# Moving the gating sort, its search and two copies in a convolution, attention and gating kernel

## The reference, cut to what matters

```
x = x + conv(groupnorm(x), w)
t = tokens(x)
# attention: 5000 nodes, 80000 random edges, 8 heads of 8
score = exp(clip(sum(k[src] * q[dst]) / sqrt(8), -5, 5))
t = t + segsum(v[src] * score, dst) / (segsum(score, dst) + 1e-6)
# gating: 8192 tokens, 262144 random edges, 4 heads x 4 experts
h = x @ W_gat;  e = leaky_relu(a_src[src] + a_dst[dst]);  alpha = softmax of e over each dst
agg = segsum(h[src] * alpha, dst);  gate = softmax(top2(mean_heads(layernorm(agg))))
t = t + sum_e gate[e] * (gelu(t @ W1[e] + b1[e]) @ W2[e] + b2[e])
```

## Time and profile before

| | |
|---|---|
| median of 3 executions | 2664.83 us |
| profiled execution, its own time | 2667.64 us |
| profiled execution, span of its instructions | 2665.8 us |
| VectorE busy | 1932.1 us (72%) |
| GpSimd busy | 1769.0 us (66%), issuing DMAs |
| TensorE busy | 1203.0 us (45%) |
| ScalarE busy | 535.9 us (20%) |

### The profile page before, as it was taken

The page is one execution under the profiler, slowest core; times in us unless marked ns, Lnnn a source line. Parts: engine busy times, 40 slices in busy tenths (PEclk is TensorE's granted clock), DMA queues, the critical chain, the costliest instruction groups (busy, mean ns, idle before and its releaser), DMA issues.

```text
span 2665.8 us, 34021 instructions
## 1 busy us (share of the span) xinstructions
PE 1203.0 (45%) x12499; PEld 1007.2 (38%) x12499; DVE 1932.1 (72%) x3127; ACT 535.9 (20%) x640; POOL 1769.0 (66%) x1690
## 2 busy tenths in 40 slices
PE   3874000000001001010214399589889898898286
PEld 2532000000000000000113255379889898887266
DVE  7588596988687878787888501168888888888356
ACT  1010002222222223131201011222222222222121
POOL 0001877777777777774677677777777777777470
PEclk9976555555555555555555555579989899899658
DMA  9500213233333333231222706112121222221101
GB/s 299 193 1 23 72 38 106 86 118 101 98 105 93 107 94 115 86 116 50 70 75 51 97 6 186 23 25 25 24 40 25 39 25 25 40 25 24 30 9 33
DMA packets 145715, 186.75 MB, mean 70 GB/s; under 512 B 84845, under 2 KB 103983, under 8 KB 139167
## 3 DMA queue, kind: packets, MB, share of 16 engines
q1 hardware_dynamic: 91494, 121.12, 14.6%
q0 software_dynamic: 54080, 63.61, 13.9%
HBM read 97.32 MB, written 87.32 MB: 69 GB/s over the span
## 4 chain that ended last, share of the span: by engine, by line
POOL 60%; issue 20%; DVE 10%; PE 6%; DMA 1%; ACT 1%; SPq 1%; POOLq 0%; DVEq 0%
POOL arena L729 56%; DVE arena L1359 7%; PE psum L933 2%; POOL d_adseed L816 2%; POOL d_qseed L753 1%; PE psum L1095 1%; SPq L569 1%; DVE arena L1362 1%; PE psum L1126 1%; PE psum L1011 1%; DVE psum L1761 1%; PE psum L1023 1%; ACT arena L1201 0%; DVE arena L1782 0%; DVE arena L1764 0%
## 5 line engine op out<-in xcount | busy, mean ns | idle before, releaser
L1359 DVE TENSOR_TENSOR arena<-arena 128x512 f32<-128x512 f32 (+18 forms) x1347 | 802.8, 635 | 160.7 <-ACT arena L1165 53.1
L729 POOL DMA_INDIRECT arena<-d_h,arena x668 | 696.4, 1042 | 203.7 <-issue 203.4
L729 POOL DMA_INDIRECT arena<-in_kv,arena x640 | 648.1, 1013 | 199.0 <-issue 194.5
L1050 PE MATMUL psum<-arena 128*128 128x128 bf16 x10080 | 613.6, 224 | 92.6 <-DVEq L1969 90.6
L1050 PEld LDWEIGHTS psum<-arena 128*128 128x128 bf16 x10080 | 600.1, 100 | 97.2 <-DVE arena L1362 94.9
L849 PE MATMUL psum<-arena 128*128 128x128 f32 (+3 forms) x402 | 90.0, 391 | 1100.2 <-DVEq L1435 1004.1
L849 PEld LDWEIGHTS psum<-arena 128*128 128x128 f32 (+3 forms) x402 | 68.7, 202 | 1122.7 <-DVEq L1435 1019.3
L1362 DVE TENSOR_SCALAR arena<-arena 128x512 bf16<-128x512 f16 (+9 forms) x1067 | 339.6, 376 | 67.7 <-ACT arena L1265 24.6
L1359 DVE TENSOR_TENSOR arena<-psum,arena 128x512 f32<-128x512 f32 (+2 forms) x179 | 167.2, 942 | 207.8 <-PE psum L1011 202.6
L729 POOL DMA_INDIRECT arena<-d_adst,arena x40 | 54.4, 1360 | 257.5 <-DVEq L1606 245.6
L1761 DVE TENSOR_TENSOR_SCAN psum<-psum,arena 128x1024 f32<-128x1024 f32 x40 | 91.9, 2298 | 137.0 <-ACT arena L1188 136.0
(11 more groups left out here) (184 smaller groups left out, 1385.5 us busy)
## 6 DMA issues: line engine op xcount, KB each, us to landing
d_gs<-arena SPq DMA_DIRECT2D x32, 768.0 KB
d_as<-arena SPq DMA_DIRECT2D x20, 1152.0 KB, 4.5
d_qseed<-arena SPq DMA_DIRECT2D x5, 4096.0 KB, 29.8
arena<-d_qseed SPq DMA_DIRECT2D x20, 1024.0 KB, 6.0
arena<-d_h,arena POOLq DMA_INDIRECT x668
arena<-in_kv,arena POOLq DMA_INDIRECT x640
d_adseed<-arena SPq DMA_DIRECT2D x1, 4096.0 KB, 29.4
arena<-d_adseed SPq DMA_DIRECT2D x17, 128.0 KB
```

The lines of the kernel that those rows point to most:

```text
L729: return pool.indirect_dma_start(out, None, table, bass.IndirectOffsetOnAxis(index[:, t:t + 1], 0))
L1050: last = nc.tensor.matmul(ps[2 + turn_of(b, m)][:, k * PICK_W:(k + 1) * PICK_W], pick_hot[turn_of(b, m)][:, t, k * P:(k + 1) * P], h_split ...
L1359: return V.tensor_tensor(o, a_, b_, op)
```

## The change

1. `SORT_EACH` goes from 14.5 to 22.0 and `LAY_TAKES` from 4.5 to 9.0, so that the sort ends before `lay` of chunk 18; the step `sorted` (unpack the list, histogram, running counts) stands there now, on VectorE and TensorE.
2. SyncE stores the gating list right after its loop, ahead of the last two chunks' rows; inside the loop it loads the next indices after `a_used` alone, and waits for `a_rows_set` and stores rows after that.
3. GpSimd does groups 0 and 1 of the search (32 of 64 gathers) ahead of its wait for the last attention rows.
4. In the attention loop ScalarE copies k into `a_prod` and v into `a_msg` feature-major; VectorE's products read these, and `a_used` is given by ScalarE's second copy.
5. In the gating loop (all chunks but the first) keep factors and weights lie in PSUM (`g_keep`, `g_weight`); ScalarE does one more exponential for the weights.
6. `g_found` and `g_below` lie elsewhere in SBUF.

The numbers that set the order, and the place of `sorted`:

```
-FIRST_CHUNK, SORT_EACH, LAY_TAKES, WEIGH_TAKES, TAILS_AFTER, CARRIES_AFTER = 60.0, 14.5, 4.5, 1.0, 4.0, 10.0
+FIRST_CHUNK, SORT_EACH, LAY_TAKES, WEIGH_TAKES, TAILS_AFTER, CARRIES_AFTER = 60.0, 22.0, 9.0, 1.0, 4.0, 10.0
...
+        if not steps and ("sorted", None) not in order:
+            order.append(("sorted", None))
```

The tiles in PSUM, and SyncE's attention loop and what follows it:

```
+        g_keep = psum[:, 4 * 512:4 * 512 + G_F * G_COLS]
+        g_weight = psum[:, 7 * 512:7 * 512 + G_HEADS * G_COLS]
...
                     sp.wait_ge(a_used, it * 2 + (b + 1))
-                    sp.wait_ge(a_rows_set, it * 2 + (b + 1))
-                    sp.dma_start(out_v[bass.ds(it * 2 + b, 1)].rearrange("c p j f -> (c p) j f"), a_rows[b]).then_inc(a_rows_out[b], 16)
                     nxt = it * 2 + (b + 2)
...
                     sp.dma_start(q_seed[b], seed_v[bass.ds(nxt, 1)].rearrange("c p j f -> (c p) j f")).then_inc(a_seed_in[b], 16)
+                    sp.wait_ge(a_rows_set, it * 2 + (b + 1))
+                    sp.dma_start(out_v[bass.ds(it * 2 + b, 1)].rearrange("c p j f -> (c p) j f"), a_rows[b]).then_inc(a_rows_out[b], 16)
+            sp.wait_ge(g_list_set, 1)
+            for out, src in ((d_gsrc, g_key[1 - G_LAST]), (d_gdst, g_key[G_LAST]), (d_gdlong[1:], g_key[G_LAST])):
+                sp.dma_start(out.rearrange("(p j) -> p j", p=P), src.bitcast(I32)).then_inc(g_list_out, 16)
```

GpSimd after its attention loop:

```
+            pool.wait_ge(run_set, 2)
+            pool.wait_ge(g_list_out, 64)
+            for group in (0, 1):
+                g_search(group)
+
             for b in range(2):
                 pool.wait_ge(a_rows_out[b], 16 * (A_CHUNKS // 2))
...
-            for group in range(4):
+            for group in (2, 3):
                 g_search(group)
```

ScalarE, `lay` of the attention and `weigh` of the gating:

```
                 act.wait_ge(kv_in[b], (c // 2 + 1) * 16 * (A_RUN + 1))
-                nc.scalar.copy(by_f[:, :, 0], q_first[b]).then_inc(a_laid, 1)
+                nc.scalar.copy(by_f[:, :, 0], q_first[b])
+                nc.scalar.copy(a_prod.rearrange("p (f j) -> p f j", j=A_RUN), kv[b][:, :, 0:CH].rearrange("p j f -> p f j")).then_inc(a_laid, 1)
+                nc.scalar.copy(a_msg[:, 0:CH * A_RUN].rearrange("p (f j) -> p f j", j=A_RUN), kv[b][:, :, CH:].rearrange("p j f -> p f j")).then_inc(a_used, 1)
...
+                keep = g_keep if back else g_corr_f
+                if back:
+                    nc.scalar.activation(g_weight, g_em, ACT.Exp)
                 nc.scalar.activation(g_msg[:, G_HF * G_COLS:], g_em, ACT.Exp).then_inc(g_exp_done, 1)
-                nc.scalar.activation(g_corr_f[:, G_HF * G_COLS:], g_dm, ACT.Exp).then_inc(g_exp_done, 1)
+                nc.scalar.activation(keep[:, G_HF * G_COLS:], g_dm, ACT.Exp).then_inc(g_exp_done, 1)
```

VectorE, `score`, `weighted_sum` and the gating's `weighted_sums`:

```
-                    step(tt(a_prod[:, at].rearrange("p (f j) -> p f j", j=A_RUN), q_edge.rearrange("p (f j) -> p f j", j=A_RUN),
-                            k_f[:, half * HALF_F:(half + 1) * HALF_F], ALU.mult))
+                    step(tt(a_prod[:, at], q_edge, a_prod[:, at], ALU.mult))
...
+                dve.wait_ge(a_used, c + 1)
                 dve.wait_ge(a_weighed, c + 1)
...
-                        kv[c % 2][:, :, CH:].rearrange("p j (h d) -> p h d j", d=A_DIM),
+                        a_msg[:, 0:CH * A_RUN].rearrange("p (h d j) -> p h d j", d=A_DIM, j=A_RUN),
                         bc(w[:, :, None, :], [P, A_HEADS, A_DIM, A_RUN]), ALU.mult))
-                dve.sem_inc(a_used, 1)
...
-                w = g_msg[:, G_HF * G_COLS:].rearrange("p (h j) -> p h j", j=G_COLS)[:, :, 1:]
+                w = (g_weight if back else g_msg[:, G_HF * G_COLS:]).rearrange("p (h j) -> p h j", j=G_COLS)[:, :, 1:]
...
-                link(it, b, back, V.tensor_tensor_scan(g_sum, g_corr_f, g_msg, 0.0, ALU.mult, ALU.add))
+                link(it, b, back, V.tensor_tensor_scan(g_sum, g_keep if back else g_corr_f, g_msg, 0.0, ALU.mult, ALU.add))
```

More of the change, by code:

```diff
@@ L210, in interleaved @@
         left = sort_for(rest) if rest > 0 else rest
[L211 to L216, removed]
+    assert not steps and order.index(("sorted", None)) < order.index(("lay", A_CHUNKS - 1))
+    return order + [("tails", None), ("carries", None)]
 SORT_AND_ATTEND = interleaved()
@@ L443, in build @@
         assert g.at <= a_key_at + 2 * A_ROOM
-        gs_ = Region(g_mid)
-        g_found = gs_.take(NT * P, I32).rearrange("p (n j) -> p n j", j=P)
+        gs_ = Region(g_mid - 16 * P)
+        g_found = Region(g_mid + 2048).take(NT * P, I32).rearrange("p (n j) -> p n j", j=P)
         g_below = gs_.take(16 * P).rearrange("p (n j) -> p n j", j=P)
@@ L633, in _ @@
             sp.dma_start(d_ac.rearrange("(c p) f -> p c f", p=P), a_car).then_inc(a_car_out, 16)
[L636 to L639, removed]
             sp.wait_ge(a_car_out, 16)
@@ L778, in _, with g_search @@
                     a_gather_first(b)
+            g_list_rows = d_gdst.rearrange("(n j) -> n j", j=P)
+            def g_search(group):
+                for t in range(16 * group, 16 * group + 16):
+                    gather_rows(g_found[:, t, :], g_list_rows, g_nodes.run_i, t).then_inc(found[1][group], 16)
+            pool.wait_ge(run_set, 2)
+            pool.wait_ge(g_list_out, 64)
+            for group in (0, 1):
+                g_search(group)
             for b in range(2):
@@ L980, in _ @@
                     a_carries()
-            pe.wait_ge(hot_set, 2)
-            histogram(G_W // P)
-            running(2, g_nodes)
+                elif what == "sorted":
+                    pe.wait_ge(hot_set, 2)
+                    histogram(G_W // P)
+                    running(2, g_nodes)
             for n in range(8):
@@ L1250, in weigh @@
                 nc.scalar.copy(g_msg.rearrange("p (f j) -> p f j", j=G_COLS)[:, :, 0], before_sum if back else zeros[:, 0:G_F])
-                nc.scalar.copy(g_corr_f[:, 0:G_HF * G_COLS].rearrange("p (h k j) -> p h k j", h=G_HEADS, j=G_COLS),
-                               bc(g_corr_f[:, G_HF * G_COLS:].rearrange("p (h j) -> p h j", j=G_COLS)[:, :, None, :],
+                nc.scalar.copy(keep[:, 0:G_HF * G_COLS].rearrange("p (h k j) -> p h k j", h=G_HEADS, j=G_COLS),
+                               bc(keep[:, G_HF * G_COLS:].rearrange("p (h j) -> p h j", j=G_COLS)[:, :, None, :],
                                   [P, G_HEADS, G_EXP, G_COLS])).then_inc(g_weighed, 1)
```

2 lines of the change are left out of this document (1 added, 1 removed).

## The result

The kernel after takes 2620.52 us (median of 4 executions, 2618.04 to 2622.83) against 2665.34 for before on the same chip (4 executions, 2663.48 to 2666.10): ratio 0.9835, interval 0.9823 to 0.9847. It is faster by 45 us, or 1.6%, inside the range of 2573 to 2632; but 70 us were forecast. (Before's profiled execution took longer than any of its other four, after's is the fastest of its own.)

What follows compares the result with a forecast made beforehand. The prediction took GpSimd (its gathers, waits and slowdowns) to bound the kernel. 2667.6 - 48 (up to the last search gather) - 18 - 5 (gating loop) = 2597 us profiled, 2595 as median; range 2573 to 2632.

Steps and rivals of the forecast that it cites:

- index wait: Attention loop, chunk 2: GpSimd's 4.13 us wait for an index load goes, -4 us.
- wait for the last attention rows: After the attention loop: GpSimd's 35.49 us standstill, filled with 32 search gathers, disappears, -35.5 us.
- wait for the gating list: GpSimd's 1.57 us wait goes because the list is stored earlier, -1.6 us.
- GpSimd under the sort, in the loop: Attention loop: the sort moved into it stretches GpSimd's gathers, +15 us, bounds +8 and +24.
- the same, between the loops: Between the loops: 22 us lost beside the sort go, carry gathers meeting the normalization add 6, -16 us.
- 64 searches: Search gathers: 94 us before, now 41 for the first 32 and 46 for the others, -7 us.
- last search to its count: End of the search: allowance for VectorE's count after the last gather, turning -49 into -48 us.
- gating loop: GpSimd holds VectorE: Gating loop's end: VectorE's waits of 1.83, 1.79 and 16.08 us for GpSimd, whose gathers get shorter, -18 us.
- gating loop: faster product: Gating loop: VectorE's product gets faster, -5 us.
- the first rival: Attention loop becomes VectorE's, at 46 us a chunk from chunk 5 to 17, 23 us more: 2618 us; chance 13%.
- The second rival: Gating loop: gathers stay long, GpSimd keeps 49.4 us a chunk, -18 and -5 are lost: 2618 us; chance 12%.
- The slower one: Attention loop: ScalarE's copies of k and v take 9 us or more each, about 2690 us; chance 4%.

## Why the prediction was partly right

Each term as the prediction had it, against the profiled executions:

| step | forecast | measured |
|---|---|---|
| index wait | -4 | -4.1 |
| wait for the last attention rows | -35.5 | -35.5 |
| wait for the gating list | -1.6 | -1.6 |
| GpSimd under the sort, in the loop | +15 | +20.8 |
| the same, between the loops | -16 | -10.6 |
| 64 searches | -7 | -5.8 |
| last search to its count | +1 | +3.4 |
| gating loop: GpSimd holds VectorE | -18 | -14.9 |
| gating loop: faster product | -5 | 0 |
| tail | 0 | -1.1 |

The measured ones add up to -49.4 (a start 0.5 earlier not counted), the profiled difference is -49.6. The forecast of 70 was too high by 25 in the medians. It is within the range because that was wide. Five terms were mis-sized (the loop under the sort, the stretch between the loops, the searches, the last landing and the gating loop), and one, the product, was wrong.

**What held.** The three waits went, and nothing took their place: the first run-end gather has 0.30 ahead of it. GpSimd sets the attention loop, not VectorE, so the first rival was not what happened; it does come true in the kernel with split compares and VectorE's own reads of k and v. There GpSimd by itself would need no more than the 42.5 us a chunk that it takes with the split compares alone (44.5 in after), and it waits 34.5 us. The second rival is out: the gathers in the gating loop are 0.94. The slower one is out too: the copies take 3.77 and 3.71 us. The Trainium skill (SBUF — State Buffer, "Who interferes with whom") says that a VectorE instruction with two SBUF inputs contends with a GpSimd instruction that reads SBUF. The trace agrees, if issuing a gather counts as one that reads: 2.40 us beside the product with two SBUF inputs, 0.94 with one in PSUM. It speaks against the section's inference, for these gathers, that making descriptors needs the write side only. Whether making the descriptors or reading the indices in SBUF is what waits, no run here tells.

**The loop under the sort, +15 for +20.8.** Two parts of this term were wrong. I took it below the 17 that the loop's own rate gave, arguing that "the attention's own product no longer falls in with strided SBUF reads". The kernel in which VectorE reads k and v has the same loop as after, 455.45 to 1256.88, so that saved nothing. And the rate was taken per microsecond of sort, when what a gather loses depends on how long the one instruction beside it is: cut in two, the same compares let the loop lose 765.0 - 18 x 41.5 = 18 us, against 801.7 - 747 = 55 in after. Two thirds of the loss come from the length. The rows of before already had the reason: the gathers beside product and scan end at 2072.74 and 2075.76, each 0.75 us after that instruction's end.

**Between the loops, -16 for -10.6, and 7 for 5.8.** I counted 6 us lost, by the carry gathers alone, under the normalization. 80 gathers in 111.6 us are 11.6 over 80 x 1.25, so the step that failed is the 6. Which of VectorE's instructions stretch them was not tested.

**The last landing, +1 for +3.4.** I took the last group to have landed right behind its gather. In the view by DMA queues of after, 1430 to 1470 us (packets, MB, share of 16 engines; then KB, median us to landing):

```profile
q1 hardware_dynamic: 16448, 0.79, 65.9%
...
d_h<-arena SPq DMA_DIRECT2D x2, 320.0 KB, 12.2
arena<-d_gdst,arena POOLq DMA_INDIRECT x20, 6.1
```

The stores of h and of its scores, in packets of 48 bytes on average, fill the DMA engines and hold up a gather of 64 KB. Moved behind the search, the count starts 2.54 us after the last gather does, as in before, where it was 5.97 in after. Before had the same 16448 packets beside its search, but issued them at 1462.22, 32 us ahead of its last gather, and they were all but gone by 1490. After issues them at 1440.51, 17 us ahead of the last gather. The change brought the last gathers forward by 37 us and the stores by only 22. The step that failed is that I looked at which engine issued last, and not at what else was in the DMA engines. The +3.4 is also the least that any profile here shows: in the seven other kernels with this search and these stores the count came 7.3 to 10.8 us after the gather.

**The gating loop, -18 for -14.9.** The mechanism was right, and undone and done alone it gave 10.5 and 15 us. The term was too large: I took all but 1.5 us of the three waits as gain. Of the 16.08, 2.25 are left, and the last waits for TensorE's picks in this chunk grew from 0.50 and 3.09 to 2.47 and 3.50, so some 11 came out of it; the two chunks before gave 2.6 of the 3.6 us in their waits.

**The product, -5 for 0.** This step was wrong. I carried 1.76 ns an element over from the attention's product to the gating one. That product reads v at a stride of 128 floats; this one reads h at a stride of 20, and takes 2.29 us whether its weights lie in SBUF or in PSUM. With h laid out contiguously it takes 1.22: the order of the reads costs 1.07 us, the second SBUF input nothing. (A compare of 1024 contiguous floats, both inputs in SBUF, takes 1.23.) Why a stride of 20 costs more than one of 128 was not tested. The gain of 5 was there to be had (16 even), by the edit that the attention loop got and the gating loop didn't.

## What to carry to other kernels

Where GpSimd's indirect DMAs set the pace, look at how long each of VectorE's instructions with two SBUF inputs is, not only at how much of them there is: put one operand in PSUM, or cut them. A wait that is filled with work from later on pays in full only if the landings behind that work are free too; read the DMA view at the place where the new last transfer lands. And a copy by an idle engine is worth what the engine it relieves is worth: nothing while another one sets the loop (put into before alone, the copies even cost 4 us), 26 us once that other one is faster.

## What the runs showed of the hardware

- A gather that GpSimd issues beside a compare of 1024 floats with both inputs in SBUF took 1.77 us, beside ones of 512 1.23, and 0.94 beside none. Beside the product (2.29 us) and the scan (2.87) it ended 0.75 us after they did. All gathers of k and v rows average 1.036 us in after and 0.984 with the compares split.
- VectorE's time for a product of 1024 floats: 1.22 contiguous, 1.88 at a stride of 128 floats, 2.29 as the gating loop reads h (a stride of 20); the last didn't change with its other input moved from SBUF to PSUM.
- 16448 packets of 0.79 MB in all took 66% of the 16 DMA engines for 40 us. Gathers beside them landed in 6.1 us by the median, and in 2.5 in the same stretch of the kernel with the stores moved; the count behind the last one started 5.97 to 10.84 us after it, and 2.54.
- TensorE's granted clock was 0.50 in the first microseconds behind its wait of 4.47 us for VectorE and 1.00 later; 96 matmuls took 7.15 to 8.18 us there, and 5.52 at 1.00.
